# Chunk 1 of the first weights and tokens asked for from the activation engine's DMA queue

## The reference

```python
base = einsum('btd,od->bto', x, W)
logits = einsum('btd,ed->bte', x, Wr) + one_hot(language_ids) * 5.0
topw, topi = top_k(logits, 2)
gates = sum(one_hot(topi) * softmax(topw)[..., None])
h = einsum('btd,erd->bter', x, A)
out = x + base + 2.0 * einsum('bter,bte,eor->bto', h, gates, B)
```

## Time and profile before

| what | us |
|---|---|
| median of three runs | 80.47 |
| lowest, highest | 80.07, 80.56 |
| the profiled execution's own time | 80.74 |
| its span (first to last instruction) | 78.9 |
| TensorE matmul busy (PE) | 75.4 (95%) |
| VectorE busy (DVE) | 48.8 (62%) |
| ScalarE busy (ACT) | 22.1 (28%) |
| GpSimd busy (POOL) | 22.6 (29%) |
| bytes moved | 14.23 MB |

### The profile page before, as it was taken

How to read it: one execution, slowest core, us unless ns; L and a number is a source line. 1 busy time by engine, 2 the same in 40 slices (tenths; PEclk the granted TensorE clock), 3 DMA queues, 4 the chain that set the end, 5 groups by cost and what they waited for, 6 DMA issues and landing times.

```text
span 78.9 us, 1629 instructions
## 1 busy us (share of the span) xinstructions
PE 75.4 (95%) x505; PEld 71.4 (90%) x505; DVE 48.8 (62%) x220; ACT 22.1 (28%) x56; POOL 22.6 (29%) x26
## 2 busy tenths in 40 slices
PE   6999999999999999999999999999999999999960
PEld 2388799899999999999999999999999999999950
DVE  0095695888892828466482928275664829787750
ACT  4423961244231414050231314140503214112100
POOL 4032926061550241406050513305060605100000
DMA  1999995389199289999930000270000053031133
GB/s 12 293 263 362 412 425 237 40 324 408 37 252 423 121 224 428 423 282 349 411 143 6 0 0 0 97 302 0 0 0 0 0 249 149 0 133 77 60 133 133
DMA packets 3892, 14.23 MB, mean 180 GB/s; under 512 B 432, under 2 KB 1328, under 8 KB 3632
## 3 DMA queue, kind: packets, MB, share of 16 engines
q1 hardware_dynamic: 3744, 13.98, 48.4%
q10 hardware_dynamic: 144, 0.20, 0.7%
HBM read 9.99 MB, written 4.19 MB: 180 GB/s over the span
## 4 chain that ended last, share of the span: by engine, by line
PE 87%; DMA 7%; SPq 1%; ACT 1%; DVE 1%; issue 0%
PE heads_ps L421 43%; PE base_ps L421 28%; DMA first_sb<-in_first 7%; PE heads_ps L453 5%; PE base_ps L453 5%; PE base_ps L457 2%; PE heads_ps L457 2%; PE ghT_ps L444 2%; ACT x_hi L231 1%; SPq L165 1%; DVE out_sb L337 1%; SPq L164 0%; PE warm_ps L444 0%
## 5 line engine op out<-in xcount | busy, mean ns | idle before, releaser
L206 POOL TENSOR_TENSOR x_lo<-xT_sb,x_hi 128x512 fp32r<-128x512 f32 x14 | 18.1, 1294 | 38.8 <-ACT x_hi L241 37.0
L421 PE MATMUL heads_ps<-w_hi,x_hi 128*128 128x392 f32 x64 | 22.8, 366 | 0.2 <-ACT x_hi L231 0.2
L421 PE MATMUL heads_ps<-w_hi,x_lo 128*128 128x392 f32 x64 | 21.6, 348 | 0.0
L421 PE MATMUL heads_ps<-w_lo,x_hi 128*128 128x392 f32 x64 | 21.1, 339 | 0.0
L421 PE MATMUL base_ps<-w_hi,x_lo 128*128 128x256 f32 x64 | 17.8, 281 | 0.0
L421 PE MATMUL base_ps<-w_hi,x_hi 128*128 128x256 f32 x64 | 17.8, 289 | 0.0
L421 PE MATMUL base_ps<-w_lo,x_hi 128*128 128x256 f32 x64 | 17.4, 280 | 0.0
L287 DVE TENSOR_TENSOR ghT_lo<-ghT_ps,ghT_hi 128x128 fp32r<-128x128 f32 x15 | 4.4, 291 | 14.8 <-ACT ghT_hi L245 14.7
L421 PEld LDWEIGHTS heads_ps<-w_hi,x_hi 128*128 128x128 f32 x64 | 12.0, 192 | 1.2 <-ACT x_hi L231 0.7
L421 PEld LDWEIGHTS heads_ps<-w_hi,x_lo 128*128 128x128 f32 x64 | 12.0, 191 | 0.5 <-POOL x_lo L210 0.5
L245 ACT ACTIVATE ghT_hi<-ghT_ps 128x128 fp32r<-128x128 f32 x15 | 4.1, 275 | 29.5 <-PE ghT_ps L444 29.5
(11 more groups left out here) (43 smaller groups left out, 92.2 us busy)
## 6 DMA issues: line engine op xcount, KB each, us to landing
x_sb<-in_x SPq DMA_DIRECT2D x4, 768.0 KB, 5.5
out<-out_sb SPq DMA_DIRECT2D x4, 768.0 KB, 4.4
xT_sb<-in_xT SPq DMA_DIRECT2D x3, 768.0 KB, 4.3
first_sb<-in_first SPq DMA_DIRECT2D x3, 454.0 KB, 5.8
xT_sb<-in_xT SPq DMA_DIRECT2D x1, 1024.0 KB, 6.3
x_sb<-in_x SPq DMA_DIRECT2D x1, 1024.0 KB, 9.6
out<-out_sb SPq DMA_DIRECT2D x2, 256.0 KB, 2.0
out<-out_sb SPq DMA_DIRECT2D x4, 128.0 KB, 1.7
```

Source lines behind the costliest of these rows:

```text
L206: nc.gpsimd.tensor_tensor(x_lo[:, s, :], xT_sb[:, t - len(FIRST), :], x_hi[:, s, :].bitcast(FP32), ALU.subtract).then_inc(x_lo_made, 1)
L421: return nc.tensor.matmul(dst, xs[:, s, chunks[k]], ws[:, k, cols], start=(k == 0 and n == 0), stop=(k == KC - 1 and n == last_n))
```

## The change

The request for c1 is taken out of SyncE's loop and put into the activation engine's stream, right behind the request for wh0 and ahead of the wait for `x_landed`. Destination, source and semaphore stay, and so does everything that waits for them.

```diff
-            for k in range(1, KC):
+            for k in range(2, KC):
                 sp.dma_start(first_sb[:, k, :], first[:, k, :]).then_inc(chunk_landed[k - 1], 16)
             load_xT(2, 1, xT_third)
...
             act.dma_start(w_sb[:, 0, heads_cols], w[:, 0, heads_cols]).then_inc(wh_landed, 16)
+            act.dma_start(first_sb[:, 1, :], first[:, 1, :]).then_inc(chunk_landed[0], 16)
             act.wait_ge(x_landed, 16)
             chunk_upper(0)
```

## The result

The changed kernel takes 79.72 us, the median of 10 runs (79.5 to 80.24), against 80.42 us of the kernel before in 10 runs (79.97 to 80.99; the first three runs are among them). The medians differ by 0.70 us. The ratio is 0.993, with a 95% interval of 0.9904 to 0.9957: 0.7% faster, small but clear of no change. (The ratio is taken over the fast runs of both kernels alone, so it needn't equal the quotient of the medians.) In two later comparisons it was 0.9947 (0.9922 to 0.9972) and 0.9943 (0.9911 to 0.9974), where the medians lay 0.50 and 0.13 us apart; the direction holds in all three, the size less so. The forecast was 80.5 us, in a range of 79.8 to 81.8; the measured median lies 0.08 us under the lower end of the range.

What follows compares the result with a forecast made beforehand. TensorE, busy 75.4 of 78.9 us, was taken as the bound, with c1's landing setting the start. Parts 3, 2, 6 and 7 each came to 0, so 80.5 us, the median of before, in a range of 79.8 to 81.8.

Steps and rivals of the forecast that it cites:

- rival A: The forecast itself: c1 lands within 0.3 us of 6.8, wb0 at 4.9 to 6.0, hidden; 80.5 us; chance 0.50.
- rival B: c1 lands earlier by its 0.5 us of earlier request: 80.0 us, at most the 0.75 bound, 79.7; chance 0.14.
- rival D: TensorE waits for chunk 0's base weights (late wb0): 81.3 us at T = 6.8, 81.7 with the clock; chance 0.20.
- Parts 1 and 2: ScalarE's stream: c1 issued at about 1.18, 0.5 us earlier; table load behind it at 1.6 to 2.9, cost 0.
- Part 3: Worth of c1's earlier request: DMA engines are the limit, landing at best 0.35 us earlier; gain taken as 0.
- Part 4: Queue sharing: turns packet by packet, so wb0 is served with c1 and lands at 4.9 to 5.3 instead of 4.1.
- Part 5: Slow DMA stretch (203 GB/s, 4.5 to 5.5): if it recurs, wb0 lands between 4.9 and 6.8; 5.6 taken.
- Part 6: Cost of late wb0 on TensorE: cover until it lands at 5.95; cost 0 at 5.6, 0.85 us at 6.8.
- The bound of 0.75 us: Most an earlier c1 can give: chunk 1's second x_lo pair at 8.0 instead of 8.76, 0.9% of 80.47.
- Its own signs: Profile checks: x_hi of chunk 1 at 6.5 to 7.1, second x_lo pair 8.5 to 9.0; wrong before 8.2 or after 9.5.
- Its second price: Rival D's clock part: TensorE's wait delays its upper level, 2.0 us at most, about 1.2 if halfway; half of D's chance.

Runs made afterwards that it cites:

- reorder_alone: The kernel before with only TensorE's reordering (chunk 0's two x_lo heads matmuls ahead of the wait for base weights), c1 still on SyncE's queue: 80.37 us, ratio 1.0028.
- c2_on_act: Against the kernel before: c2 instead of c1 goes to the activation engine's queue behind wh0, c1 stays behind wb0: 80.61 us, ratio 1.0071.
- balanced: Against the changed kernel: c1 cut in three, tokens and base weights on the activation engine's queue, head weights on SyncE's: 80.2 us, ratio to before 0.9973.
- late_request: Against the changed kernel: c1's request held until GpSimd has written a marker tile, going out at 1.57, same queue: 79.91 us, ratio to before 0.9989.
- sp_c1_first: Against the changed kernel: c1 back on SyncE's queue but ahead of wb0, asked for at 1.19: 80.31 us, ratio to before 1.0023.
- swap_wb0: Against the changed kernel: wb0 and c1 change queues, wb0 on the activation engine's, c1 on SyncE's: 80.36 us, ratio to before 1.0034.
- x_lo_first: Against the changed kernel: TensorE does chunk 0's two x_lo heads matmuls before waiting for the base weights: 79.39 us in six runs, ratio to before 0.9861.
- hold_requests: Against the kernel before: SyncE waits for c1's landing before requesting tile 2's tokens and all that follows: 80.2 us, ratio 1.0007.
- heads_before_base: Against the changed kernel: TensorE does chunk 0's other four heads matmuls (w_lo, x_lo) before waiting for the base weights: 79.83 us, ratio to before 0.9945.

## Why the prediction was wrong

The time forecast was that of rival A. What happened on c1's side was rival B, at its full bound, with a part of rival D's mechanism on wb0's side.

- *Parts 1 and 2 were right.* c1's issue came at 1.18, the table load at 1.67 to 2.95 under its cover.
- *Part 3 failed.* It took c1's landing as unchanged, at most 0.35 us earlier, since the engines' busy share of 0.94 to 1.10 was read as full, and it gave the request, asked for 0.5 us earlier, no worth. c1 landed 1.4 us earlier between the first two traces, and 0.8 to 1.1 earlier against the others of before and reorder_alone. The share was high because packets took long, not because many bytes moved: 203 GB/s at 0.94, 419 at 1.03, with single packets of up to 1.06 us in the first and 0.14 us in the second. The 316 to 358 GB/s around it were short of the full rate too.
- *Part 4 was right in its mechanism.* Turns by packet put wb0 at 4.8 to 5.3 in three traces, where 4.9 to 5.3 was worked out (the 5.3 is one late engine's, a mild form of what part 5 feared), and c2_on_act shows the same from the other side. The rule of the Trainium skill on whole packets of many descriptors ("DMA: Bandwidth & Descriptors", Queues, rings and completion order) doesn't describe this: by it wb0 would have stayed near 4.1.
- *Part 5 failed,* and with it the price of the gain. It saw the slow stretch and took it for a property of that time, which would come again and catch wb0. It came in the five traces with one queue (203 to 334 GB/s), in none of seven with two (410 to 429), and in a milder form in balanced (330) and late_request (374), also with two. The rule of the Trainium skill quoted in part 3 ("DMA: Bandwidth & Descriptors", Issuing engines are not separate DMA queues), that several issuing engines save only issue time, was read there as no gain. The runs show a gain of 0.5% to 0.7%. Since c1's earlier request is issue time saved, the gain alone doesn't speak against the rule; the rates do, as far as they go.
- *Part 6 was right in its mechanism,* but its cover was counted against a start of the x_lo pair at 8.76. With c1 at 5.4 chunk 2 could start at 5.4 + 2.96 = 8.4, so wb0 counts from 8.4 - 3.8 = 4.6 on, not from 5.95. It landed at 4.8 to 5.3 and gave back 0.2 to 0.9 us of the gain, the most in the third trace. The bound of 0.75 us on the whole fits the medians, which moved by 0.70, and the x_lo pair, for which 8.0 was worked out as the earliest, came at 7.97. But it was no bound on a single execution: it rested on chunk 0's loads of one trace, ending at 6.96. In the second trace of after they end at 6.75, and chunk 2 starts at 8.58, 1.17 us ahead of the first trace of before.
- *Its own signs showed it.* x_hi of chunk 1 at 5.39 is the sign of B (6.3 or earlier), and the x_lo pair at 7.97 is before the 8.2 from which the forecast was to be called wrong.
- *Rival D* had TensorE wait for the base weights. It does, in all three traces, by 0.3 to 0.9 us of idle loads. The third trace shows the low level lasting into chunk 0's base work, at 0.3 us or so. It wasn't the end on the slower side because c1's gain was larger. Its second price, the level held back by the wait, came in part in the third trace only.

What is shown and what is argued: that an earlier c1 is what starts chunk 2 earlier, and that wb0's landing then sets it, is shown by the 11 traces that the two rules fit, by sp_c1_first and swap_wb0, where an early c1 with a late wb0 won nothing, and by x_lo_first beside reorder_alone. Why c1 lands earlier isn't shown. The second queue goes with the higher DMA rate, for another chunk too (c2_on_act), but not without exception (balanced, late_request), and the rate stayed high from 5.0 on, when the second queue had hardly a packet left; c1's landing goes better with the time of its request and its place among the others. Of the runs only late_request sets the one against the other, in one trace. Why single packets take up to 1 us is open too: hold_requests excludes the writing of later requests, but nothing was tried on the size of packets or on where the data lie in memory.

## What to carry to other kernels

A busy share near 1 in the DMA engines isn't a full rate: read GB/s beside it, and look for a landing that comes long after the bytes must be through. Where the first loads decide, it can be worth trying to ask for the late one earlier from a second queue, as here; of the four orders tried with two queues beside after's, none was faster. When a late transfer is won back, the next one to be waited for (here wb0) has lost its cover; reorder the consumer so that it does what is ready, as x_lo_first did.

## What the runs showed of the hardware that was not expected

- With all early loads but wh0 in one queue the rate from 4.5 to 5.5 us was 203 to 334 GB/s in five traces, with one of them in the second queue 410 to 429 in seven, 374 and 330 in two more, at shares of 0.90 to 1.06 in all of them. A busy share near 1 therefore stood for half the rate once and for the full rate another time.
- c1's landing in one queue, asked for at 1.66 behind wb0, varied from 5.8 to 6.8 in four traces; in after, asked for at 1.18, from 5.4 to 5.5 in three.
- Two queues take turns by single packets: from 3.5 to 4.0 in after 46 packets (0.16 MB) started in one and 53 (0.05 MB) in the other; c2, in the second queue, overtook c1 (5.6 against 6.7) while wb0 slipped from 4.1 to 5.0.
- TensorE's loads reached their short length at different moments in executions with the same start: from the first load of chunk 0 at 4.45 in after, from chunk 0's base work at 5.26 in its second trace, after 6.2 in its third, though the granted clock reads 1.00 in these stretches.
- VectorE's w_lo of 128x392 took 1.04 us for one while GpSimd made x_lo of chunk 0 beside it (from 4.33 in sp_c1_first); the eight w_lo operations of before, of both sizes, range from 0.41 to 1.07 with a median of 0.62. That the two engines hold each other up is likely but wasn't tested. The late w_lo is what heads_before_base ran into.
